# Cross-attention keys stacked in four groups of four heads, and a feed-forward whose probabilities are turned three steps behind their scores

## The reference, cut to what matters

```python
x = _layernorm(x + _L0_attn_ref(x, ...))            # 16 heads of 128, causal, tanh softcap, gates
x = _layernorm(x + _L0_xattn_ref(x, ctx_2048, ...)) # 16 heads of 16, 1444 keys a batch, 8-bit linears for q and o
x = _layernorm(x + _L0_ffn_ref(x, ...))             # a causal attention of 16 heads of 16 steers a gated MLP
```

```python
# cross-attention, a batch at a time
k = (cond @ wk.T + bk).reshape(B, L, H, D).transpose(0, 2, 1, 3)
scores = jnp.einsum('bhnd,bhld->bhnl', q, k) * inv_sqrt_d + mask[:, None]
attn = jax.nn.softmax(scores, axis=-1)
# feed-forward
x = _rmsnorm(hidden_states, ln1_w)
attn = _attention(x, Wq, Wk, Wv, Wo)          # scores, causal softmax, values, Wo
mod = 0.1 * jnp.tanh(attn @ A)
h = _rmsnorm(residual, ln2_w)
gate = jax.nn.silu(h @ W_in_base.T + mod * (h @ A) @ B)
mlp_out = gate * (h @ W_up_base.T) @ W_down.T
return residual + mlp_out
```

## Time and profile before

| | |
|---|---|
| three runs | 3964.13, 3969.43, 3971.38 us (median 3969.43) |
| the profiled execution | 3973.11 us, of which 3971.4 us from its first to its last instruction (the span) |
| granted TensorE clock, mean | 0.925 |
| busy: PE, DVE, ACT, POOL | 3606.3, 2420.2, 1700.7, 629.0 us |
| busy: PE weight loads | 2673.7 us |

### The profile page before, as it was taken

How to read it: one execution, slowest core, us unless ns; L and a number is a source line. 1 busy time by engine, 2 the same in 40 slices (tenths; PEclk the granted TensorE clock), 3 DMA queues, 4 the chain that set the end, 5 groups by cost and what they waited for, 6 DMA issues and landing times. The chain is left out here.

```text
span 3971.4 us, 94397 instructions
## 1 busy us (share of the span) xinstructions
PE 3606.3 (91%) x34556; PEld 2673.7 (67%) x34556; DVE 2420.2 (61%) x5690; ACT 1700.7 (43%) x2883; POOL 629.0 (16%) x664
## 2 busy tenths in 40 slices
PE   7999999995899999998999999999999968888887
PEld 6989899895566666665666666566666636666666
DVE  4444444445576776766767676676766746665565
ACT  3222232222455554554545555454555534333332
POOL 0000000002111111111101111011111102333222
PEclk9999999997999998999989999898998978988999
DMA  3000000001554646464564646546464521000000
GB/s 98 14 13 12 4 8 12 12 9 41 96 110 85 125 84 120 77 121 88 89 115 81 121 84 106 105 84 119 76 122 87 97 48 41 13 12 12 21 12 13
DMA packets 122425, 257.11 MB, mean 65 GB/s; under 512 B 19140, under 2 KB 99852, under 8 KB 118972
## 3 DMA queue, kind: packets, MB, share of 16 engines
q1 hardware_dynamic: 113744, 244.11, 32.7%
q10 hardware_dynamic: 8300, 7.69, 0.7%
HBM read 99.95 MB, written 9.83 MB: 28 GB/s over the span
## 5 line engine op out<-in xcount | busy, mean ns | idle before, releaser
L1385 DVE CUSTOM_DVE_ANT_0 ca_rowmax<-ca_rowmax,ca_msk 100x420 f32<-100x420 f32 (+1 forms) x1024 | 923.9, 926 | 577.3 <-PE ca_rowmax L1168 572.0
L1109 ACT ACTIVATE ca_prob<-ca_unit 128x800 f32<-128x800 f32 x768 | 640.3, 834 | 466.3 <-PE ca_unit L1292 464.8
L1168 PE MATMUL ca_rowmax<-ca_ks,ca_qs 96*100 96x512 bf16 (+1 forms) x1536 | 535.2, 427 | 92.5 <-DMA ca_ks<-ca_ks 68.0
L1292 PEld LDWEIGHTS ca_unit<-ca_qs,ca_ks 99*128 99x128 bf16 (+1 forms) x6144 | 385.0, 104 | 250.7 <-issue 169.9
L1292 PE MATMUL ca_unit<-ca_qs,ca_ks 99*128 99x100 bf16 (+1 forms) x6144 | 463.2, 220 | 31.1 <-issue 16.4
L1255 PE MATMUL ca_acc<-ca_prob,ca_vaug 128*17 128x100 f32 x12288 | 469.4, 269 | 16.5 <-issue 9.1
L1002 POOL TENSOR_TENSOR ca_key_part<-ca_key_rest,ca_key_part 128x512 bf16<-128x512 f32 (+1 forms) x192 | 209.9, 1100 | 1594.8 <-ACT ca_key_part L1064 1594.8
L1150 PE MATMUL ca_ring<-ca_wvT,ca_ctxT 128*128 128x256 f32 (+1 forms) x1536 | 381.6, 390 | 3.2 <-DVE ca_key_rest L1359 1.6
L1141 PE MATMUL ca_ring<-ca_ctxT,ca_wkT 128*128 128x512 f32 (+1 forms) x768 | 345.9, 573 | 2.4 <-DVE ca_key_rest L1359 2.4
L1168 PEld LDWEIGHTS ca_rowmax<-ca_ks,ca_qs 96*100 96x100 bf16 x1536 | 166.2, 133 | 250.6 <-issue 177.6
L1255 PEld LDWEIGHTS ca_acc<-ca_prob,ca_vaug 128*17 128x17 f32 x12288 | 247.4, 101 | 118.4 <-issue 53.7
(11 more groups left out here) (275 smaller groups left out, 6252.1 us busy)
## 6 DMA issues: line engine op xcount, KB each, us to landing
ca_ks<-ca_key_part SPq DMA_DIRECT2D x768, 90.2 KB, 4.1
ca_ks<-ca_ks SPq DMA_DIRECT2D x64, 722.0 KB, 7.4
ca_ctx<-in_ctx SPq DMA_DIRECT2D x32, 1408.0 KB
ca_ks<-ca_ks SPq DMA_DIRECT2D x64, 361.0 KB, 9.4
ca_msk<-in_mask_BxSxS_ff SPq DMA_DIRECT2D x32, 564.1 KB
sa_w_stage<-in_L_attn_w_qkv SPq DMA_DIRECT2D x12, 512.0 KB, 5.2
sa_x_in<-in_x ACTq DMA_DIRECT2D x8, 400.0 KB
sa_x_res<-in_x SPq DMA_DIRECT2D x8, 400.0 KB
```

Source lines behind the costliest of these rows:

```text
L1109: act.activation(prob[:, 2 * (p % 2):2 * (p % 2) + 2, :], unit[:, :, 0:QUAD * N], ACT.Exp)\
L1168: last = pe.matmul(rowmax[0:N, s0:s1], qs[0:STACK, par, h, :], ks[0:STACK, par, h, s0:s1], start=True, stop=True)
L1292: return pe.matmul(unit[0:rows(t0 + k), k, j * N:(j + 1) * N], ks[:, par, h, keys(k)], qs[:, par, h, :], start=(j == 0), stop=True, skip_g ...
L1385: dve.tensor_tensor_reduce(rowmax[0:N, s0:s1], rowmax[0:N, s0:s1], msk[:, par, s0:s1], 1.0, -3.0e38, ALU.add, ALU.max, top[:, bank, h:h + ...
```

## The change

Two edits that have nothing to do with each other.

In cross-attention `HALF` (8 heads, two stacks) becomes `GROUP` (4 heads, four stacks). The same 24 puts are issued, each of 90.2 KB; the four repeat DMAs of a batch become eight, each of half the size. The two pairs of semaphores are kept and counted on by twos (`group % 2`). The context load now stands behind the repeat of group 2, and PE waits at heads 0, 4, 8 and 12.

```diff
-    HALF = H // 2
+    GROUP = QUAD
+    GROUPS = H // GROUP
...
+        def wait_stacked(eng, group, b):
+
+            eng.wait_ge(stacked[group % 2], STACKED * (GROUPS // 2 * b + group // 2 + 1))
...
+                def put(group):
+
+                    for part in range(PARTS):
                         standing_wait(sp, (hi_out, mid_out, parts_out)[part], 6 * (b + 1), sp_passed)
-                        for n in range(half * HALF // C, (half + 1) * HALF // C):
+                        for n in range(group * GROUP // C, (group + 1) * GROUP // C):
...
+                def repeat(group):
+
+                    heads = slice(group * GROUP, (group + 1) * GROUP)
+                    standing_wait(sp, placed[group % 2], PLACED * (GROUPS // 2 * b + group // 2 + 1), sp_passed)
+                    if group >= 2:
+                        wait_stacked(sp, group - 2, b)
+                        sp.sem_inc(sp_passed, 1)
...
-                put(0, (0, 1, 2))
-                put(1, (0,))
+                put(0)
+                put(1)
                 repeat(0)
-                put(1, (1, 2))
+                put(2)
+                repeat(1)
+                put(3)
+                repeat(2)
                 if more:
 
                     bn.wait_full(sp, ("ct", 2, C - 1), b)
                     sp.sem_inc(sp_passed, 1)
                     load_ctx(b + 1)
-                repeat(1)
+                repeat(3)
...
-                    if kind == "mh" and h % HALF == 0:
-                        pe.wait_ge(stacked[h // HALF], STACKED * (b + 1))
+                    if kind == "mh" and h % GROUP == 0:
+                        wait_stacked(pe, h // GROUP, b)
```

```diff
+    TURN = 3
+    STEPS = UNITS + TURN + 1
+    between = {u: ("up", u) for u in range(UNITS)}
+    between |= {UNITS + n: t for n, t in enumerate((("gate", 0), ("gate", 1), ("gate", 2), ("ua",)))}
...
+                for step in range(STEPS):
+                    if step < UNITS:
+                        scores_of(g, step)
+                    u = step - TURN
                     if 0 <= u < UNITS:
                         pe.wait_ge(prob_done, UNITS * g + u + 1)
+                        turned(g, u, 0)
+                    name, *which = between[step]
+                    if name == "up":
+                        project(g, ("up", step), up_s, hT, step)
+                    elif name == "gate":
+                        gate(g, *which)
+                    else:
+                        ua(g)
                     if 0 <= u < UNITS:
+                        turned(g, u, 1)
+                    if u >= 1:
+                        weighted(g, u - 1)
+                gate(g, 3)
+                for b in range(G - 2, G):
+                    bk.wait_out(pe, ("o", b), g)
...
+                gate(g, 5)
+                pe.wait_ge(w_done, g + 1)
+                for f in range(6):
+                    gate_end(g, f)
+                for f in (6, 7):
+                    gate(g, f)
+                    gate_end(g, f)
+                if more:
+                    turn_normed(g + 1)
                 for n in range(G // 2):
                     bank = bk.bank(("down", n))
```

The next group's transposes (`turn_normed`) thus come ahead of this group's down projection, and their high and low parts are made beside it (ACT's `highs(g + 1)` behind its tanhs, DVE's `lows(g + 1)` behind `gated`). `ua` shares bank 6 with the attention output `o` of batches 0 and 2 of the group, so it waits for DVE's copy of batch 2. The other engines:

```diff
@@ gpsimd
+                if before:
+                    finish(g - 1)
                 for step in range(UNITS + 1):
...
                 if more:
                     start(g + 1)
-                if before:
-                    finish(g - 1)
+                for f in range(FC):
+                    pool.wait_ge(gated_done, FC * g + f + 1)
+                    pool.tensor_tensor(hid[:, f, :], gated[:, f % 2, :], up[:, f, :], ALU.mult).then_inc(hid_done, 1)
@@ scalar
+                for n in range(G // 2):
+                    bank = bk.bank(("v", n))
+                    bk.wait_full(act, ("v", n), g)
+                    act.activation(v[:, 2 * n:2 * n + 2, :, :],
...
+                        evacuate(act, up[:, step, :], ("up", step), g, scale=0.5)
@@ vector
-                for n in range(G // 2):
-                    bank = bk.bank(("v", n))
-                    bk.wait_full(dve, ("v", n), g)
-                    dve.tensor_copy(v[:, 2 * n:2 * n + 2, :, :],
...
+                if before:
+                    finish(g - 1)
+                for step in range(STEPS):
...
+                    if more and step == UNITS + 1:
+                        start(g + 1)
+                    u = step - TURN - 1
                     if 0 <= u < UNITS and u % C == C - 1:
                         b = u // C
                         bank = bk.bank(("o", b))
                         dve.wait_ge(pv_done, UNITS * g + u + 1)
...
+                    if f >= 2:
+
+                        dve.wait_ge(hid_done, FC * g + f - 1)
                     dve.scalar_tensor_tensor(gated[:, f % 2, :], half_tanh[:, f % 2, :], 1.0, ps[bank][:, 0:T],
                                              ALU.add, ALU.mult).then_inc(bk.freed[bank], 1)
                     bk.wait_out(dve, ("gate", f), g)
-                    dve.scalar_tensor_tensor(hid[:, f, :], gated[:, f % 2, :], 0.5, up[:, f, :], ALU.mult, ALU.mult)\
-                        .then_inc(hid_done, 1)
+                    dve.sem_inc(gated_done, 1)
+                if more:
+                    lows(g + 1)
```

More of the change, by code:

```diff
@@ L1582, in rows_of, with run_groups @@
             return w.rearrange("(c p) n -> p c n", p=P)
[L1584 to L1587 removed]
+        def run_groups(eng, group, begin, finish=lambda g: None):
+            begin(0)
             group(0, True, False)
@@ L1708, in square, with highs @@
                 act.activation(squares[:], x[:, b, :], ACT.Square, accum_out=ssq[:, b:b + 1]).then_inc(squared, 1)
-            def start(g):
-                load(g)
-                high_parts(0, FIRST)
-                for b in range(G):
-                    square(g, b)
-            def group(g, more, before):
+            def highs(g):
                 for name, dst in (("xt", xT), ("ht", hT)):
@@ new lines, in group @@
+            def group(g, more, before):
+                for c in range(C):
+                    bk.wait_out(pe, ("xt", c), g)
+                if not before:
+                    pe.wait_ge(w_lows, FIRST)
+                for c in range(C):
+                    project(g, ("k", c), wk_s, xT, c)
+                for c in range(C):
+                    project(g, ("q", c), wq_s, xT, c)
+                values(g)
+                pe.wait_ge(w_lows, len(halves) + 1)
+                for step in range(STEPS):
+                    if step < UNITS:
+                        scores_of(g, step)
+                    u = step - TURN
@@ L2004, in group @@
                             .then_inc(bk.freed[bank], 1)
-                if more:
-                    start(g + 1)
-                if before:
-                    finish(g - 1)
                 bk.wait_out(dve, ("ta",), g)
```

246 lines of the change are left out of this document (108 added, 138 removed).

## The result

The kernel after takes 3752.14 us (median of four runs, 3750.40 to 3757.66), the kernel before beside it 3970.4 (3964.13 to 3976.74): ratio 0.945, 95% interval 0.943 to 0.947. The forecast's sum was 3773, or 3769 beside the median; its range went from 3696 up to the first rival's 3889. The profiled execution took 3757.66 us with a span of 3755.9, against 3973.11 and 3971.4: 215 us less, where the steps had made 200.

A forecast was written before the change was run, and what follows sets the result against it. PE sets the pace in cross-attention, but below full clock behind its waits for repeat copies; feed-forward gaps are chains ended by other engines. 3973.1 - 150 (cross-attention) - 50 (feed-forward) = 3773 us, 3769 beside the median; own range 3700 to 3830.

The forecast's parts named there:

- first rival: Cross-attention: context load lands at +40.4, PE waits at L1214 and the clock falls; turn 68.5 us, 3889 us, chance 0.16.
- A turn thus pays twice for the wait: Cross-attention, repeat copies: some 2.2 us for the wait itself and, in most turns, 3.8 us for the slow clock behind it.
- The wait at head 0 goes, with 2 to 7 us to spare: Cross-attention: the first repeat lands at +13.6 to +18.5, PE comes to its `mh` at +20.4.
- a tie: Cross-attention: context load lands at +38.5 (+35.6 to +40.2), needed at +38.8; one more half-size repeat pair ahead costs 4.0 us.
- The 0.6 us of missed loads and the 0.5 of clock: Cross-attention, charges per turn: 0.6 us for turns missing the context load, 0.5 where a miss brings the slow clock back.
- Rivals 1 and 2: Cross-attention: context load late at +40.4 (3889 us, chance 0.16), or at +44 with turns of 72.1 us (4001, chance 0.05).
- The pace: Feed-forward, first scores to DVE's scaling of the last unit's: from 25.2 us to 22.4, -2.8 a group.
- third step of lag: Feed-forward: three steps of lag let PE go on while POOL's product is late; -2.8 us a group.
- The tail's new gap: Feed-forward: PE waits about 2.4 us before `ua` for DVE's copy of `o`, behind the normed rows; tail +4.5 us a group.
- `hid` on POOL at no cost: Feed-forward: 0.8 us a product, eight end 8 us behind `w_done`, `down` wants the last near 8.2; -0.4 us may go.
- The third: Feed-forward gives nothing: the new gap before `ua` and the clock behind it eat the savings; 3819 us, chance 0.16.
- The fourth: Cross-attention: the wait at head 0 is not for the copies' size or place; 3919 us, chance 0.03.

The follow-up runs named there:

- the wait put back: Kernel after, with PE at head 0 also waiting for group 1's repeat, which it doesn't read yet: 3928.90 us, ratio 0.988 to the kernel before.
- the order alone: Kernel before, with the four early puts of half 1 moved behind the repeat of half 0, repeats full-size: 3898.50 us, ratio 0.982.
- The load put last: Kernel after, with the context load moved behind the repeat of group 3 too: 3763.26 us, ratio 0.947 to the kernel before.
- the layout without it: Kernel after with `TURN = 2` for 3, probabilities turned a step earlier and gate 2 behind the loop: 3788.84 us, ratio 0.955 to the kernel before.
- the edit alone: Kernel before with only the new feed-forward, cross-attention as before: 3924.49 us, ratio 0.989.
- the four stacks alone: Kernel before with only the four key stacks in cross-attention, feed-forward as before: 3798.85 us, ratio 0.957.

## Why the prediction was right, step by step

**The bound.** "A turn thus pays twice for the wait", 2.2 us for itself and 3.8 for the clock: shown by the wait put back (a gap of 2.57, 69.10 us) against after (63.40). Taking the wait away gave both.

**The wait at head 0 goes, with 2 to 7 us to spare.** It went, with 5 (+15.3 against +20.4). The times were right, one reason was not: I let the issue of sixteen puts set the repeat's time. It is the landing of its own twelve that sets it: by the medians the twelfth has landed at +12.9 before and at +11.6 with the order alone, and the repeat is issued 0.1 us behind it in both. That the repeat follows right behind the twelve puts at +8.8 (the median after) held only because a group of four waits for six, and that was luck. Had the edit been the order alone, my working would have promised most of the gain, and it brings 68 us of 168. I costed DVE at nothing at head 0 and didn't ask about the heads behind it: with the wait gone, PE's waits for DVE's row maxima grow from 16.1 us in all (28 of them) to 33.1 (69), half a microsecond a turn.

**The context load, "a tie".** The step that was mis-sized. I charged 4.0 us for one more pair ahead of it and read a landing of +38.5. By the packets it lands some 2 us later than before, and by the rate at +35 to +36. It isn't issued later: before, a full pair and 24 puts were out by +24.5 (1367.91); after, three small pairs and 24 puts by +23.9 (1345.23). The small copies run beside puts that SP issues anyway: they hold the entries behind them up by 1.3 us at the first pair (1.86 for an issue of 0.59), where the full pair held them up by 5.7. The 0.6 us of missed loads and the 0.5 of clock were 0. With the stalls at 0.82 a turn (64.15 less the median of 63.33) for 0.47, and the ordinary turn at 63.33 for 63.05, the sum is 64.15 for 64.6. Rivals 1 and 2 rested on that same price. The load put last shows how near they were: with one pair more the load is late in every third turn, because there the pair does hold up the load's issue, by 3.5 us. So the price of 4.0 is about right for a pair that waits for its puts, and about twice too high for those that the change puts ahead of the load.

**The feed-forward**, in us (before from the earlier trace rows, forecast from the steps, after from the rows above):

| stretch | before | forecast | after |
|---|---|---|---|
| first scores to last unit's scaling | 25.2 | 22.4 | 23.7 |
| from there to `at` | 11.55 | 16.1 | 16.5 |
| `at` to `down` | 21.6 | 16.6 | 15.95 |
| `down` to next first scores | 26.2 | 23.2 | 22.4 |
| group | 84.6 | 78.3 | 78.55 |

All four are within 1.3 us. The pace is the furthest off: the gap of 1.85 at the fourth scores, DVE still scaling, was not in it. The forecast called the third step of lag worth 2.8 us; against the layout without it it is worth 5.6. The tail's new gap was priced from POOL's root and eight products and came as priced. Taking it away gave 3.4 us a group, 24 in the stage (654.2 to 630.3) and 26 by the medians; I had priced the gap at 2.5 (+2 in place of +4.5) without asking whether the rows could stand elsewhere.

**`hid` on POOL at no cost.** Right in the sum, wrong in its terms: 1.0 us a product and not 0.8, and the last ends 9.8 us behind `w_done` and not 8, so `down` does wait for the last two, 0.6 us a group. It costs nothing against DVE all the same, where the last would end no sooner. The Trainium skill's rule (GPSIMD Engine Reference, opening), that Vector is roughly twice as fast for elementwise work, is nearer, and the trace agrees: 1.04 to 0.575 is 1.8. The 22 us that the forecast had estimated by that rule didn't come (654.2 against 654.8 with `hid` on DVE), since the slower engine has only half of the chain's work and does it beside the faster one.

**The rivals.** The third (the feed-forward gives nothing) fell by the edit alone: 3924.49, 46 us less. The fourth fell by the four stacks alone (the wait is gone, cross-attention 2128.0). The first and second fell by the context load, which lands before PE comes.

## What to carry to other kernels

Count a wait in front of PE with the clock behind it: here 2 us of waiting for a copy cost 5.3 a turn, 0.6 to 1.2 us cost 2.7 in the mean, and the cheapest gain was to let the copy be smaller and wait for fewer pieces. For a DMA queue that works in order, ask what each waiting entry waits for (a landing, not an issue) before you price what moves past it. And when a gap is filled and nothing is gained, follow the chain that starts where the gap ends, and list every place where PE meets it (here a bank and the last two products): each is a bound of its own.

## What was not expected of the hardware

- The clock falls behind a gap by chance: behind 5 of 16 gaps of 0.6 to 1.2 us at head 0, 7 of 13 of 1.2 to 1.5, 22 of 24 of 1.8 to 2.2 and all 23 over 2.6. Gaps of 1.47 and 1.52 us in one trace had different outcomes.
- A transfer of half the size doesn't take half the time to land: 722.0 KB took a median of 7.4 us before, 361.0 KB 5.3 after; the second DMA of a pair 9.4 (361.0 KB) and 6.4 (180.5 KB).
- DVE's product of two tiles in SBUF takes 0.575 us with POOL idle and 0.855 (32 of them, 0.835 to 0.878) beside POOL's products, which keep their 1.03 to 1.06. DVE's `gated`, with one operand in PSUM, keeps its 0.57 beside POOL. The Trainium skill says which pairs meet (SBUF — State Buffer, "Who interferes with whom": a Vector instruction with two SBUF inputs contends with a GpSimd one that reads SBUF), and the trace agrees; that the other side is fully blocked, as the section says of the shared ports, it doesn't show: DVE's product stands beside POOL's for 0.43 us and is 0.28 longer.
- PE is idle for 1.5 to 6 us with nothing shown that it waits for, three to eight times a run in cross-attention and thirteen times with the order alone. Two of these stalls are no matter of chance: in all fourteen traces one of 4.0 to 6.2 us stands some 10 us into the twelfth full turn, and one of 3.9 to 4.7 some 9 us into the 22nd. In both, four to seven transfers of the queues that the profile calls `instruction` fall within the gap and the microsecond before it, where their mean rate gives about one. Whether PE waits for them was not tested. The stall in the twelfth turn of after:

```profile
1746.41 0.76 PE L1305 MATMUL ca_unit<-ca_qs,ca_ks 99*128 99x100 bf16 x7 [5.78 <-issue]
```
